# Norms with five and three PSUM banks and another ScalarE order, and GpSimd's query norm behind the scaling

## The reference, cut to what matters

```python
def _layernorm(x, axis=-1, eps=1e-05):
    m = jnp.mean(x, axis=axis, keepdims=True)
    v = jnp.var(x, axis=axis, keepdims=True)
    return (x - m) / jnp.sqrt(v + eps)

h = h + _L0_attn_ref(_layernorm(h, axis=-1), ...)
h = h + _L1_attn_ref(_layernorm(h, axis=-1), ...)     # four layers with two norms of their own each, with gamma and beta
h = h + _L2_ffn_ref(_layernorm(h, axis=-1), ...)      # begins with an RMS norm, which subtracts no mean
h = h + _L3_attn_ref(_layernorm(h, axis=-1), ...)
```

```python
q = _rmsnorm(_rope(q), q_norm_w)
k = _rmsnorm(_rope(k), k_norm_w)
scores = jnp.einsum('bqgtd,bqgsd->bqgts', q, k) * scale
attn = jax.nn.softmax(scores, axis=-1)
out = jnp.einsum('bqgts,bqgsd->bqgtd', attn, v)
```

## Time and profile before

| | us |
|---|---|
| median of 3 runs | 3343.57 (3341.24 to 3367.22) |
| the profiled execution, its own time | 3340.73 |
| its span in the trace | 3338.9 |
| PE busy in it | 3045.4 (91%) |
| DVE, ACT, GpSimd busy | 2144.7, 1768.1, 1174.2 |

### The profile page before, as it was taken

How to read it: one execution, slowest core, us unless ns; L and a number is a source line. 1 busy time by engine, 2 the same in 40 slices (tenths; PEclk the granted TensorE clock), 3 DMA queues, 4 the chain that set the end, 5 groups by cost and what they waited for, 6 DMA issues and landing times. The chain is left out here.

```text
span 3338.9 us, 60593 instructions
## 1 busy us (share of the span) xinstructions
PE 3045.4 (91%) x22307; PEld 1885.5 (56%) x22307; DVE 2144.7 (64%) x4177; ACT 1768.1 (53%) x3895; POOL 1174.2 (35%) x1167
## 2 busy tenths in 40 slices
PE   7999989999999999989888889996799999989999
PEld 6999857446465554357455533334466566655444
DVE  7999745016364553358568544445899999965777
ACT  1323245665756566556525433334566666655666
POOL 4666511001010011027257322223677777750000
PEclk9999989999999999999999999997899999999999
DMA  2000000000000000000000032210100000003776
GB/s 88 15 20 11 1 19 12 1 7 2 7 4 4 4 5 6 2 7 2 9 1 1 25 65 56 56 33 16 25 12 5 4 5 5 4 16 37 72 67 65
DMA packets 75645, 66.40 MB, mean 20 GB/s; under 512 B 20502, under 2 KB 70840, under 8 KB 74936
## 3 DMA queue, kind: packets, MB, share of 16 engines
q1 hardware_dynamic: 75352, 62.52, 11.0%
HBM read 55.58 MB, written 2.51 MB: 17 GB/s over the span
## 5 line engine op out<-in xcount | busy, mean ns | idle before, releaser
L707 ACT ACTIVATE p_hidden<-p_hid_ps,net_bias 128x344 f32<-128x344 f32 x816 | 382.7, 549 | 230.5 <-PE p_hid_ps L654 171.4
L680 PE MATMUL p_y_ps<-p_hidden,net_down 128*64 128x344 f32 x1632 | 287.8, 466 | 2.1 <-DVE p_hidden L756 1.9
L654 PE MATMUL p_hid_ps<-xn,net_up 64*128 64x344 f32 x1248 | 242.3, 490 | 8.1 <-PEq L316 4.6
L2785 DVE TENSOR_TENSOR p_hid<-p_silu,p_pair_ps 128x344 f32<-128x344 f32 x288 | 134.7, 509 | 172.9 <-PE p_pair_ps L2734 95.1
L756 DVE TENSOR_TENSOR p_hidden<-p_hidden,p_row 128x344 f32<-128x344 f32 x384 | 175.3, 513 | 78.3 <-ACT p_hidden L707 45.1
L2766 ACT ACTIVATE p_silu<-p_pair_ps 128x344 f32<-128x344 f32 x288 | 116.0, 454 | 201.3 <-PE p_pair_ps L2723 201.3
L1919 POOL TENSOR_TENSOR p_rot<-p_rot,p_cross 128x512 f32<-128x512 f32 x128 | 160.4, 1275 | 126.5 <-DVE p_cross L2074 126.5
L2470 POOL TENSOR_TENSOR p_qt<-p_qt,p_q_sum 97x512 f32<-97x512 f32 (+1 forms) x44 | 46.4, 1054 | 445.3 <-DVE p_q_sum L2413 445.3
L680 PEld LDWEIGHTS p_y_ps<-p_hidden,net_down 128*64 128x64 f32 x1632 | 103.7, 136 | 160.3 <-issue 49.5
L1932 POOL TENSOR_TENSOR p_prob<-p_prob,p_total 128x1024 f32<-128x1024 f32 (+1 forms) x128 | 185.5, 1470 | 12.4 <-DVE p_total L2100 12.4
L2712 POOL TENSOR_TENSOR p_weighted<-routed_hn,p_row 128x344 f32<-128x344 f32 x96 | 88.9, 946 | 262.0 <-PE p_pair_ps L2739 206.5
(11 more groups left out here) (475 smaller groups left out, 7978.2 us busy)
## 6 DMA issues: line engine op xcount, KB each, us to landing
p_row<-gated_rows SPq DMA_DIRECT2D x192, 86.0 KB, 2.9
p_row<-mark_rows SPq DMA_DIRECT2D x192, 86.0 KB, 10.6
tok_x<-in_tok_x SPq DMA_DIRECT2D x11, 384.0 KB, 3.1
out<-h SPq DMA_DIRECT2D x12, 172.0 KB, 3.4
shared_value_pairs<-shared_values SPq DMA_DIRECT2D x16, 128.0 KB, 2.5
p_swapped<-xn SPq DMA_DIRECT2D x64, 32.0 KB, 1.9
p_x<-in_tok_x SPq DMA_DIRECT2D x5, 384.0 KB, 3.1
p_kinds<-in_tok_c3w SPq DMA_DIRECT2D x1, 1280.0 KB
```

What stands on the lines that cost most here:

```text
L654: mm = pe.matmul(hid_ps[k % ring][:, 0:TILE], w_up[half(g), n, :], x[half(g), cols(t)], start=True, stop=not experts or by_rows)
L680: mm = pe.matmul(y_ps[u][half(g), 0:TILE], w_down[:, n, :], hid[k % hidden_ring][:], start=n == 0, stop=last and not experts)
L707: act.activation(hid[k % hidden_ring][:], hid_ps[k % ring][:, 0:TILE], func, bias=b_up[:, n:n + 1]).then_inc(act_done.sem, 1)
L2785: dve.tensor_tensor(hid[n % ring_h][g][:], silu[n % 2][g][:], c_of(n, g)[:, 0:TILE], ALU.mult).then_inc(hid_ready.sem, 1)
```

## The change: what it does

In `norm_phase` the eight banks are dealt 5 to `centered` and 3 to `var` (4 and 4 before), and the rings `square` and `rstd` have 4 places (3 before). ACT squares two tiles ahead, and then goes by `log(t)`, `squares(t + 2)`, `root(t)`; only for the first tile the root comes before the square. In the RMS norm DVE takes the squares over from ACT, three tiles ahead of the scaling. In the 16-head attention GpSimd's turn n is `scale(n - 1)`, `norm(n + 2)`, `combine(n + 3)`. All lines behind L116 move; the scaling on GpSimd, for instance, is L1932 before and L1945 after, `combine` L1919 and L1932.

```diff
--- before.py
+++ after.py
@@ -115,10 +115,10 @@
 
 def norm_phase(tower, src, dst, eps, center=True, gamma=None, beta=None, clip=None, residual=False, pos=None, loads=(), then=None):
 
-    nc, banks, ring = tower.nc, 4, 3
+    nc, banks, var_banks, ring = tower.nc, 5, 3, 4
     with phase(tower) as ph:
         centered_ps = [ph.ps(f"centered{r}") for r in range(banks)]
-        var_ps = [ph.ps(f"var{r}") for r in range(banks)]
+        var_ps = [ph.ps(f"var{r}") for r in range(var_banks)]
         square = [ph.sb(f"square{r}", [P, TILE]) for r in range(ring)]
         rstd = [ph.sb(f"rstd{r}", [P, TILE]) for r in range(ring)]
         centered = ph.counts(TILES if center else 0)
@@ -149,9 +149,9 @@
 
                 def variance(t):
                     pe.wait_ge(squared.sem, squared.at(t + 1))
-                    if t >= banks:
-                        pe.wait_ge(logged.sem, logged.at(t - banks + 1))
-                    pe.matmul(var_ps[t % banks][:, 0:TILE], tower.average[:], square[t % ring][:],
+                    if t >= var_banks:
+                        pe.wait_ge(logged.sem, logged.at(t - var_banks + 1))
+                    pe.matmul(var_ps[t % var_banks][:, 0:TILE], tower.average[:], square[t % ring][:],
                               start=True, stop=True).then_inc(var_ready.sem, 1)
 
                 for s in range(TILES + 1):
@@ -167,8 +167,7 @@
             @block.scalar
             def _(act):
                 def squares(t):
-                    if center:
-                        act.wait_ge(centered.sem, centered.at(t + 1))
+                    act.wait_ge(centered.sem, centered.at(t + 1))
                     if t >= ring:
                         act.wait_ge(var_ready.sem, var_ready.at(t - ring + 1))
                     act.activation(square[t % ring][:], values(t), ACT.Square).then_inc(squared.sem, 1)
@@ -177,24 +176,34 @@
                     act.wait_ge(var_ready.sem, var_ready.at(t + 1))
                     if t >= ring:
                         act.wait_ge(scaled.sem, scaled.at(t - ring + 1))
-                    act.activation(rstd[t % ring][:], var_ps[t % banks][:, 0:TILE], ACT.Ln,
+                    act.activation(rstd[t % ring][:], var_ps[t % var_banks][:, 0:TILE], ACT.Ln,
                                    bias=tower.eps[eps]).then_inc(logged.sem, 1)
 
                 def root(t):
                     act.wait_ge(logged.sem, logged.at(t + 1))
                     act.activation(rstd[t % ring][:], rstd[t % ring][:], ACT.Exp, scale=-0.5).then_inc(rooted.sem, 1)
 
-                for s in range(TILES + 2):
-                    if s < TILES:
-                        squares(s)
-                    if s >= 2:
-                        log(s - 2)
-                        root(s - 2)
+                for t in range(2 if center else 0):
+                    squares(t)
+                for t in range(TILES):
+                    log(t)
+                    if t == 0:
+                        root(t)
+                    if center and t + 2 < TILES:
+                        squares(t + 2)
+                    if t:
+                        root(t)
                 if then is not None:
                     act.preload_act_table(then)
 
             @block.vector
             def _(dve):
+                def squares(t):
+                    if t >= ring:
+                        dve.wait_ge(var_ready.sem, var_ready.at(t - ring + 1))
+                    dve.tensor_tensor(square[t % ring][:], src[:, cols(t)], src[:, cols(t)], ALU.mult).then_inc(
+                        squared.sem, 1)
+
                 def scale(t):
                     dve.wait_ge(rooted.sem, rooted.at(t + 1))
                     if gamma is None:
@@ -219,7 +228,11 @@
                         dve.tensor_scalar(dst[:, cols(t)], dst[:, cols(t)], -clip, clip, ALU.max, ALU.min)
 
                 two_steps = beta is not None or clip is not None or residual or pos is not None
+                for t in range(0 if center else 3):
+                    squares(t)
                 for s in range(TILES + 1):
+                    if not center and s + 3 < TILES:
+                        squares(s + 3)
                     if s < TILES:
                         scale(s)
                     if s >= 1 and two_steps:
@@ -1932,22 +1945,24 @@
                     pool.tensor_tensor(p[:], p[:], total[n % 2][:, ty, :, None].to_broadcast([P, MS, wide]),
                                        ALU.mult).then_inc(scaled.sem, 1)
 
-                for n in range(3):
-                    combine(n)
-                    norm(n)
                 def add_output(j):
                     x = acc[:, j * SEQ:j * SEQ + P]
                     r, k = place_of["y", j]
                     pool.wait_ge(t_read[r].sem, t_read[r].at(k + 1))
                     pool.tensor_tensor(x, y_sb[:], x, ALU.add).then_inc(y_added.sem, 1)
 
+                for n in range(2):
+                    combine(n)
+                    norm(n)
+                combine(2)
                 for n in range(BATCHES + 1):
                     if n >= 1:
                         for ty in (LATE, EARLY):
                             scale(n - 1, ty)
+                    if n + 2 < BATCHES:
+                        norm(n + 2)
                     if n + 3 < BATCHES:
                         combine(n + 3)
-                        norm(n + 3)
                     if n >= 4 and n % 2 == 0:
                         add_output((n - 4) // 2)
                 add_output(PAIRS - 1)
```

## The result

| | us |
|---|---|
| the changed kernel, median of 13 runs | 3322.51 (3286.73 to 3334.39) |
| the kernel before, 13 runs beside it | 3342.09 (3333.25 to 3370.57) |
| ratio, 95% interval | 0.9915 [0.9889, 0.9942] |
| profiled execution of the change: time, span, mean clock | 3334.39, 3332.6, 0.956 |

That is 20 us less, 0.85%, within the 1% that count as no change. Forecast were 3297 and 3279 to 3312: the prediction was wrong, although nearly every part of its sum came out as worked out.

The account below looks back on a forecast made before the run. Bounds taken: the norm's closed loop, 1.485 us a tile, and the attention's chain of PE, ACT and copies. Savings 39.6 + 3.2 + 3.4 = 46.2 from 3340.73 give 3294.5; with 2.8 for the median, 3297, range 3279 to 3312.

Parts of the forecast that it names:

- The centred norms: 14 norm phases: a tile falls from 1.485 to 1.18 us by the new ACT order, 39.6 us less together.
- Rival 1: Centred norms: the logarithm holds ACT 0.58 us whatever follows, no overlap; 31 us less, 3312; 14%.
- The RMS norm: RMS norm: ACT's logarithm and root bound it at 0.97 us a tile, 3.2 us less; 1.8 if DVE needs 1.1.
- The sum: Whole kernel: centred norms 39.6, RMS norm 3.2 and attention 3.4 give 46.2 us less.
- The attention: 16-head attention: removing PE's waits for GpSimd's scaling gains nothing in steady batches, only at the ends, 3.4 us.
- two alternating numbers: 16-head attention: over all 64 batches the starts alternate between 9.31 and 10.16 us apart, the even batch being longer.
- Rival 2: 16-head attention: every blocked batch gets shorter, 19 us more gained, 3278; 8%.
- rival 4: 16-head attention: GpSimd's queue becomes the bound, kernel slower; at 60% stretch 98 us on top, 3395; 4%.
- The other stages are the same instructions: All stages outside the norms and the 16-head attention: no term for them in the sum.
- rival 3: Norms and stages behind them: more phases begin at 1.2 GHz, 34 us lost if ten more norms do, 3331; 8%.

Follow-up runs that it names:

- the versions without the gap: Changed kernel and kernel before, each with 60 instead of 44 filler matmuls ahead of the half-capacity feed-forward: 3279.14 and 3330.12 us.
- the execution of the third column: The changed kernel run again without further edits, one profiled execution, in the middle of the upper group: 3322.52 us.
- 60 fillers: 60 instead of 44 PE filler matmuls ahead of the half-capacity feed-forward, in six versions; the changed kernel with it took 3279.14 us.
- a gap of 1.84 us: Changed kernel with 52 instead of 44 filler matmuls ahead of the half-capacity feed-forward: 3289.64 us, two of six runs at 3318.53 and 3323.09.
- 20 matmuls: Changed kernel with 20 instead of 12 filler matmuls ending the norm ahead of the half-capacity feed-forward, 44 fillers kept: 3285.70 us.
- the version with four and four banks: Kernel before with 60 fillers, the norms' new ACT order, DVE's RMS squares and rings of four, but banks 4 and 4: 3291.18 us.

## Why the prediction was wrong

**The centred norms: right.** The logarithm takes ACT 0.43 with work behind it (taken 0.44, bounds 0.35 and 0.58). The overlap is 0.11; "ScalarE: Activation LUTs", What ACT_TABLE_LOAD costs, in the Trainium skill says about 0.093. The tile costs 1.16, first square to last root is 14.73 (14.9). Per gamma norm 3.24 were saved (3.09), per norm without gamma 3.0 (2.85). Rival 1, no overlap, falls with this row.

**The RMS norm: right**, ACT at 0.96 a tile, 3.4 us against 3.2. DVE needs 0.96 for a square and a scaling, between its 0.9 and 1.1, so the margin was nothing. (The sum starts from 1657.57, where the row has 1657.53, which changes nothing.) **The attention: right.** Its 64 score starts span 615.87 instead of 619.24, 3.37 less (3.4): the second step is 10.90 instead of 12.60, that from batch 61 to 62 7.33 instead of 9.09, the first 0.16 longer, all others the same within 0.07. (Among these every eighth batch takes 11.04, before and after, which the prediction's two alternating numbers leave out; no term of the sum uses it.) Rival 2 falls by the equal 9.31, rival 4 by GpSimd's norm of 1.90 and its unchanged 14.02 of 19.47.

**The sum: right in size.** 46.2 forecast, 51.0 measured between the versions without the gap, 47 to 51 within each group of runs. The two norms that no longer begin at 1.2 GHz bring 2.7 us that it did not have.

**The step that failed** is the sentence "The other stages are the same instructions", and with it the weight of rival 3. The instructions are the same, their time is not. In 15 of 18 executions the clock stays at 1.2 GHz through the whole half-capacity feed-forward, behind the 3.6 us in which PE idles ahead of it, and that costs some 32 us more. The shorter norms bring this gap forward by some 29 us (40 in the execution of the third column); that it thereby meets a worse moment is the nearest reading, but no run shows it. Rival 3 had the right direction, and 3331 was nearer to the median than the forecast. But it looked for ten phases of 1.7 us each behind the norms, and held against itself that the change leaves the norms' surroundings as they are. It is one stage that the diff never touches, behind a gap that the trace of before already showed.

There was a sign beforehand: of the three times known at the outset one, 3367.22, lay 24 us above the other two, and the trace had this gap with 10 us at 1.2 GHz behind it. The range took that spread for noise; it was a second way for the same kernel to run.

What is **shown**: the gap is the cause of the two groups (none of 52 executions with 60 fillers is in an upper one; in the kernel before it is 0 of 11 against 9 of 22 on the same chip), the changed kernel meets the upper group far more often than the kernel before in the same series (10 of 13 against 3 of 13, 5 of 5 against 0 of 15), and at a gap of 1.84 us it can still happen. What is **open**: why the changed kernel does, through the moment of the gap or through something else in the work ahead of it; why the clock does not rise again in a stage in which PE has no idle time; and why the share for the same kernel differs between series (0 of 15, 9 of 22). The changed kernel with 12 and with 20 matmuls in turn on one chip would test the first. In the version with four and four banks the slower executions have the lower mean clock (0.972 at 3283.12, 0.965 at 3300.32), so its wide spread goes with the clock too; where in the program it does was not looked at.

## What to carry to other kernels

When a loop holds an engine that is not full, first look at the order of instructions on the engine that closes it: one square moved between a logarithm and its root was worth most of the 39 us (the rest are 3.4 of the RMS norm, and rings of four came with it), the fifth bank little more. Before adding up a gain, look for every idle gap of PE ahead of a long PE-bound stage and for times that fall in two groups; a change far ahead can alter how often the clock stays down behind such a gap, and this can outweigh most of the gain. Compare runs at equal mean clock, and close the gap with filler: 16 matmuls here made the kernel 43 us faster than its usual run.

## What the runs showed of the hardware

The matmuls of one stage, with PE busy throughout and the same 3.6 us gap ahead of them, ran for 80 us at 1.2 GHz or returned to 2.4 GHz after some 10, and one and the same kernel has executions of both groups (mean clock 0.968 to 0.969 and 0.956 to 0.960). I had expected the clock to return after each gap in the same way. Four matmuls of 64x344 take 1.52 us at the one level and 0.85 at the other. The fall can come after the gap: in the changed kernel run again PE had resumed at 2.4 GHz, and 1.4 us later, with PE busy without a break, the clock was at 1.2.

A wait is put down to whoever came last: 21 us of waits for GpSimd were removed, and 24 us of waits for ACT stood in their place in the same rows, with the batches no shorter by 0.01 us.
